# Attention in a macaron block: two heads of a pair on two 64-row tiles of TensorE, and another order of TensorE's work in a unit

## What is computed

```python
q = split(x @ wq.T + bq)
k = split(x @ wk.T + bk)
v = split(x @ wv.T + bv)
scores = jnp.einsum('bhsd,bhtd->bhst', q, k) / scale
scores = jnp.where(causal, scores, -jnp.inf)
weights = jax.nn.softmax(scores, axis=-1)
ctx = jnp.einsum('bhst,bhtd->bhsd', weights, v)
ctx = ctx.transpose(0, 2, 1, 3).reshape(B, S, E)
return ctx @ wo.T + bo
```

```python
x = x + 0.5 * _L0_ffn_ref(_layernorm(x, axis=-1), ...)
x = x + _L0_attn_ref(_layernorm(x, axis=-1), ...)
x = x + 0.5 * _L0_ffn_ref(_layernorm(x, axis=-1), ...)
```

## Time and profile before

| | us |
|---|---|
| median of 3 runs | 1189.49 (1185.66 to 1192.58) |
| span of the profiled execution | 1184.2 |
| TensorE, matmuls busy | 900.6 |
| VectorE busy | 636.2 |
| GpSimd busy | 553.3 |
| ScalarE busy | 487.1 |

### The profile page before, as it was taken

How to read it: one execution, slowest core, us unless ns; L and a number is a source line. 1 busy time by engine, 2 the same in 40 slices (tenths; PEclk the granted TensorE clock), 3 DMA queues, 4 the chain that set the end, 5 groups by cost and what they waited for, 6 DMA issues and landing times. The chain is left out here.

```text
span 1184.2 us, 21961 instructions
## 1 busy us (share of the span) xinstructions
PE 900.6 (76%) x7525; PEld 560.8 (47%) x7525; DVE 636.2 (54%) x1515; ACT 487.1 (41%) x767; POOL 553.3 (47%) x645
## 2 busy tenths in 40 slices
PE   2320899992048999999999799999999622999980
PEld 2320677872023454555555355555554211878770
DVE  6440333331358878878777587787876130333230
ACT  1000343340021676568645477555766301443430
POOL 2775277767510322133427234163323632577776
PEclk9999999997566999999999899999999855999995
DMA  4212676733152114131152302422200113454522
GB/s 146 66 53 84 186 187 158 179 63 28 27 158 47 43 29 149 43 79 45 32 149 67 80 18 58 136 76 63 61 17 13 46 35 113 81 114 69 87 25 19
DMA packets 101649, 92.59 MB, mean 78 GB/s; under 512 B 15348, under 2 KB 80017, under 8 KB 101521
## 3 DMA queue, kind: packets, MB, share of 16 engines
q1 hardware_dynamic: 73024, 71.71, 21.8%
q0 software_dynamic: 27136, 17.09, 10.1%
q10 hardware_dynamic: 1392, 2.51, 0.7%
HBM read 48.32 MB, written 47.12 MB: 81 GB/s over the span
## 5 line engine op out<-in xcount | busy, mean ns | idle before, releaser
L1235 DVE TENSOR_REDUCE m_units<-banks 128x2 f32<-128x512 f32 (+1 forms) x576 | 381.1, 688 | 94.3 <-PE banks L954 78.6
L1184 ACT ACTIVATE pt<-banks 128x1024 f32<-128x1024 f32 (+3 forms) x384 | 291.4, 809 | 163.3 <-PE banks L937 161.4
L954 PE MATMUL banks<-kp,qa 128*128 128x256 bf16 (+1 forms) x1536 | 229.3, 254 | 17.7 <-DMA kp<-k_stack 10.3
L1444 POOL TENSOR_SCALAR_AFFINE_SELECT pt<-pt 128x512 f32<-128x512 f32 x128 | 81.6, 638 | 256.9 <-ACT pt L1184 256.7
L937 PE MATMUL banks<-qb,kp 128*128 128x512 bf16 (+3 forms) x768 | 188.6, 329 | 7.2 <-issue 5.1
L954 PEld LDWEIGHTS banks<-kp,qa 128*128 128x128 bf16 x1536 | 119.5, 99 | 148.7 <-DVE m_units L1235 59.5
L983 PE MATMUL banks<-pt,vs 128*32 128x256 f32 (+2 forms) x2560 | 178.5, 371 | 6.1 <-POOL pt L1444 6.0
L648 ACT ACTIVATE hT<-banks,bfc 128x512 f32<-128x512 f32 (+1 forms) x192 | 113.8, 615 | 168.4 <-DVE bfc L666 94.3
L722 POOL DMA_INDIRECT mid<-ys,ids x80 | 124.9, 1561 | 70.2 <-issue 34.4
L342 POOL DMA_INDIRECT bucket<-rows,row_ix x128 | 125.7, 982 | 64.2 <-issue 38.2
L722 POOL DMA_INDIRECT out_dram<-ys,ids x80 | 123.7, 1546 | 67.8 <-DVE ys L691 32.8
(11 more groups left out here) (166 smaller groups left out, 643.1 us busy)
## 6 DMA issues: line engine op xcount, KB each, us to landing
bucket<-zero SPq DMA_DIRECT2D x16, 660.0 KB, 4.2
xb<-bucket SPq DMA_DIRECT2D x16, 660.0 KB, 4.7
q_stack<-qp SPq DMA_DIRECT2D x24, 256.0 KB, 3.0
k_stack<-kq SPq DMA_DIRECT2D x24, 256.0 KB, 3.7
qa<-q_stack SPq DMA_DIRECT2D x32, 192.0 KB, 3.5
kp<-k_stack SPq DMA_DIRECT2D x32, 192.0 KB, 4.4
qb<-q_stack SPq DMA_DIRECT2D x32, 192.0 KB, 3.4
wfc<-in_L_ffn_c_fc_dram SPq DMA_DIRECT2D x16, 256.0 KB, 3.0
```

The source lines that it names most:

```text
L954: i = nc.tensor.matmul(a_bank[a % 2][:, j * w:(j + 1) * w], qa[par][:, h, qt * P:(qt + 1) * P], kp[g][:, h // 2, k0:k0 + w], start=not dia ...
L1184: nc.scalar.activation(pt[u % PTS][:, 2 * pair:2 * pair + 2, 0:w], two[pair][:, :, 0:w], ACT.Exp, scale=SCALE).then_inc(exp_done[pair], 1)
L1235: nc.vector.tensor_reduce(m_units[:, qt, at, heads[0]:heads[-1] + 1], a_bank[a % 2].rearrange("p (h k) -> p h k", k=w), AX.X, ALU.max).the ...
L1444: nc.gpsimd.affine_select(out=v, in_=v, compare_op=ALU.is_ge, fill=0.0, base=0, pattern=[[0, HS], [1, P]], channel_multiplier=-1).then_inc ...
```

## The change

Two heads of a pair no longer use the full array one after the other with zeros in the other's rows. Each uses its own 64 rows: head s of a pair has rows 64 s to 64 s + 47 (or 50) of both operands. `qa` and `qb` shrink to one slot for a pair, with both heads in it, and their clears go (VectorE's at lines 1368 and 1371). The scores go to the same banks as before. A maxima unit now has one side (`side`, 0 or 1: the upper or lower 64 rows) and both pairs; the causal ones take two query tiles for one side. In a half the full-width ones come first, then the odd ones, then the causal ones, which so all stand in units 6, 7, 10 and 11; there are 36 as before, with as many matmuls of each width. The causal product stays a matmul on all 128 rows. TensorE's order in a unit becomes: both scores, maxima, values half 0, maxima, values half 1, maxima, maxima.

```diff
@@ AUNITS
+    HB = T // 2
     for hf in (1, 0):
-        for qt in range(hf * T // 2, (hf + 1) * T // 2):
+        qts = range(hf * HB, (hf + 1) * HB)
+        for qt in qts:
             for j in range(qt // 2):
-                AUNITS += [(qt, (0, 1), 2 * j * P, 2 * P, False, j), (qt, (2, 3), 2 * j * P, 2 * P, False, j)]
-            if qt % 2:
-                AUNITS.append((qt, range(HS), (qt - 1) * P, P, False, T // 2 - 1))
-            AUNITS.append((qt, range(HS), qt * P, P, True, T // 2))
+                for side in range(2):
+                    AUNITS.append((hf, side, [(qt, 2 * j * P)], 2 * P, False, j))
+        for side in range(2):
+            AUNITS.append((hf, side, [(qt, (qt - 1) * P) for qt in qts if qt % 2], P, False, HB - 1))
+        for q2 in range(hf * HB, (hf + 1) * HB, 2):
+            for side in range(2):
+                AUNITS.append((hf, side, [(q2, q2 * P), (q2 + 1, (q2 + 1) * P)], P, True, HB))
@@ score
-                        i = nc.tensor.matmul(two[pair][:, s, 0:w], kp[g][:, pair, kb * P:(kb + 1) * P],
-                                             qb[par][:, 2 * pair + s, q0:q0 + w], start=True, stop=True)
+                        rows_s = slice(64 * s, 64 * s + KS + 3)
+                        i = nc.tensor.matmul(two[pair][:, s, 0:w], kp[g][rows_s, pair, kb * P:(kb + 1) * P],
+                                             qb[par][rows_s, pair, q0:q0 + w], start=True, stop=True)
@@ maxima
-                        for j, h in enumerate(heads):
-                            i = nc.tensor.matmul(a_bank[a % 2][:, j * w:(j + 1) * w], qa[par][:, h, qt * P:(qt + 1) * P],
-                                                 kp[g][:, h // 2, k0:k0 + w], start=not diag,
+                        rows_s = slice(64 * side, 64 * side + KS)
+                        todo = [(qt, k0, pair) for qt, k0 in segs for pair in range(HS // 2)]
+                        for j, (qt, k0, pair) in enumerate(todo):
+                            i = nc.tensor.matmul(a_bank[a % 2][:, j * w:(j + 1) * w],
+                                                 qa[par][rows_s, pair, qt * P:(qt + 1) * P],
+                                                 kp[g][rows_s, pair, k0:k0 + w], start=not diag,
@@ TensorE's step
+                        for pair in range(2):
+                            score(par, g, b, n, u, pair)
                         for i in range(4):
-                            if i < 2:
-                                score(par, g, b, n, u, i)
-                            elif u >= LAG:
-                                values(par, n, u - LAG, i - 2)
-                            elif not (bt.first and g == 0):
-                                values(1 - par, n - 1, NU - LAG + u, i - 2)
                             if more and a0 + i < a3:
                                 maxima(n + 1, ng, nb, a0 + i, a0 + i + 1)
+                            if i > 1:
+                                continue
+                            if u >= LAG:
+                                values(par, n, u - LAG, i)
+                            elif not (bt.first and g == 0):
+                                values(1 - par, n - 1, NU - LAG + u, i)
@@ VectorE, before attention
-                nc.vector.memset(qa[0][:], 0.0)
                 norm(0)
-                for t_ in qa[1:] + qb:
-                    i = nc.vector.memset(t_[:], 0.0)
-                i.then_inc(cleared, 1)
```

More of the change, by code:

```diff
@@ L748, in macaron_block_kernel @@
             sba = maker(part)
-            qa = [sba(f"qa{i}", [P, HS, S], bf16) for i in range(2)]
-            qb = [sba(f"qb{i}", [P, HS, S], bf16) for i in range(2)]
+            qa = [sba(f"qa{i}", [P, HS // 2, S], bf16) for i in range(2)]
+            qb = [sba(f"qb{i}", [P, HS // 2, S], bf16) for i in range(2)]
             kp = [sba(f"kp{i}", [P, HS // 2, S], bf16) for i in range(NG)]
@@ L830, in load_q @@
                 def load_q(dst, b, g, done):
-                    load_stack(lambda s: dst[64 * s:64 * s + KS].rearrange("p (i s) n -> p s i n", s=2)[:, s],
-                               q_stack, b, g, done)
+                    load_stack(lambda s: dst[64 * s:64 * s + KS], q_stack, b, g, done)
                 def load_k(b, g):
@@ L880, in move @@
                     for s in range(2):
[L881 to L884, removed]
+                        src = max_rows[hf * 3 * HS:(hf + 1) * 3 * HS, :].rearrange("(c s i) n -> s c i n", c=3, s=2)[s]
+                        dst = qb[par][64 * s + KS:64 * s + KS + 3]
+                        sp.dma_start(dst[:, :, hf * HALF:(hf + 1) * HALF], src).then_inc(max_ld[hf][par], 16)
                 def store_stacks(b):
@@ L914, in _ @@
                 wait_apart(sp, stack_st, STORES)
-                wait_apart(sp, cleared, 2)
+                wait_apart(sp, cleared, 1)
                 load_q(qa[0], 0, 0, qa_ld[0])
@@ L944, in maxima @@
                     for a in range(a0, a1):
-                        qt, heads, k0, w, diag, _ = AUNITS[a]
+                        _, side, segs, w, diag, _ = AUNITS[a]
                         if a == 0:
@@ L952, in maxima @@
                                              start=True, stop=False)
-                        for j, h in enumerate(heads):
-                            i = nc.tensor.matmul(a_bank[a % 2][:, j * w:(j + 1) * w], qa[par][:, h, qt * P:(qt + 1) * P],
-                                                 kp[g][:, h // 2, k0:k0 + w], start=not diag,
-                                                 stop=not diag or j == len(heads) - 1)
+                        rows_s = slice(64 * side, 64 * side + KS)
[4 more added lines that the diff above has]
+                                                 kp[g][rows_s, pair, k0:k0 + w], start=not diag,
+                                                 stop=not diag or j == len(todo) - 1)
                         i.then_inc(a_full, 1)
@@ L1099, in _ @@
                     norm_task(pro_at, name, 0)
-                pe.wait_ge(cleared, 2)
+                pe.wait_ge(cleared, 1)
                 maxima(0, 0, 0, 0, NA1 + 4)
@@ L1232, in reduce @@
                 def reduce(n, a):
-                    qt, heads, k0, w, diag, at = AUNITS[a]
+                    hf, side, segs, w, _, at = AUNITS[a]
+                    qt, apart = segs[0][0], segs[-1][0] - segs[0][0]
+                    if apart == 2:
+                        dst = m_units[:].rearrange("p (t o) c h -> p t o c h", o=2)[:, qt // 2:qt // 2 + 2, qt % 2, at]
+                    else:
+                        dst = m_units[:, qt:qt + apart + 1, at]
                     dve.wait_ge(a_full, NA * n + a + 1)
-                    nc.vector.tensor_reduce(m_units[:, qt, at, heads[0]:heads[-1] + 1],
-                                            a_bank[a % 2].rearrange("p (h k) -> p h k", k=w), AX.X,
+                    nc.vector.tensor_reduce(dst[:, :, 2 * side:2 * side + 2],
+                                            a_bank[a % 2].rearrange("p (t h k) -> p t h k", h=2, k=w), AX.X,
                                             ALU.max).then_inc(a_done, 1)
                     if a in (NA1 - 1, NA - 1):
-                        hf = int(a < NA1)
                         wait(dve, parts_ok, 2 * n - hf)
```

## The result

The changed kernel takes 1353.3 us (median of 5 runs, 1342.1 to 1380.3) against 1189.5 us: a ratio of 1.132 (95% interval 1.127 to 1.137). I had forecast 1197.5 us, in a range of 1165 to 1238. The profiled execution is one of the longer ones, with a span of 1373.2 us.

The account below looks back on a forecast made before the run. The attention stage was taken as bound by TensorE's stream, VectorE next. Terms -59 + 14 + 34 + 17 + 7 - 5 - 0.5 make about +8 on 1189.5 us: 1197.5 us, range 1165 to 1238.

Parts of the forecast that it names:

- the last rival: TensorE's clock falls, from more gaps and half its rows idle in the maxima; no time given, chance 0.02.
- Term D: Maxima units, VectorE's cadence: TensorE waits for reductions to free maxima banks, +17 us, bounds +5 to +30.
- E: Chain behind half 1's last maxima unit: TensorE stands still before the transposition of m_parts ending unit 8, +7 us.
- Term A: Attention scores: two 64-row tiles run beside each other, halving the scores' time, -59 us, bounds 0 and -59.
- G: Clears: four clears of 1.76 us leave VectorE, -0.5 us, between -0.8 and 0.
- the rival without overlap: The two score matmuls do not overlap, wanting the same moving or weight path: +47, 1237 us, chance 0.10.
- B: Units 6, 7, 10, 11: value halves split by a maxima unit, four more column-tile visits a group, +14 us.
- C: TensorE's changes between full array and 64-row tiles: 311 new ones at 0.11 us, +34 us, bounds 0 to +44.
- The rival with free changes: Changes between full array and row tiles cost nothing: 1168.5 us, chance 0.18.
- The rivals of slow weight loads: Maxima units: loads slower in a 64-row tile, 1225 us, chance 0.07; or never hidden beside the same rows, 1313, 0.03.
- term F: Today's waits of TensorE for VectorE, mostly at causal maxima of units 8 and 9: half goes away, -5 us.

Follow-up runs that it names:

- e1: The changed kernel with all score and maxima matmuls back on the full array, its new order kept: 1214.2 us, 1.019 of the kernel before.
- e2: The changed kernel with only the maxima back on the full array, scores in row tiles, order kept: 1203.8 us, 1.011 of the kernel before.
- e3: The changed kernel with only the scores back on the full array, maxima in row tiles, order kept: 1260.2 us, 1.061 of the kernel before.
- g1: The changed kernel unaltered, run again on another chip: 1322.3 us, 1.110 of the kernel before.
- e4_fill: The changed kernel plus six unread full-array matmuls of 512 columns before each of 32 waits for m_parts: 1256.7 us, 1.055 of the kernel before.

## Why the prediction was wrong, point by point

**The step that failed is the last rival.** "The clock falls, as TensorE has more gaps and half of its rows idle in the maxima" had a chance of 0.02 and, unlike its neighbours, no time: "each 10 us at half clock costs 5" was never multiplied out, and the sum has the clock at nothing. The reason I gave against it was that "its stalls there are as long as those of terms D and E". I compared single stalls, and the stalls did stay short. What changed is that three things came together: scores in half the time, maxima on half of the rows, and more draining and waiting in units 6 to 8. In the stage the clock is at 0.98 with the last alone (e1) and at 0.96 with it and one of the others (e2, e3); with all three it is 0.65, and 0.72 in g1's profile (380 to 1078 us). That the combination does it is shown; which property of TensorE's work the clock answers to is not.

**What the clock is worth.** Three estimates, all from the runs above and none a run itself. The first is from the changed kernel alone. Its nine runs go from a span of 1276 us at a mean clock of 0.828 to 1379 us at 0.733, which is 439 to 736 us at the lower level (twice what the mean lacks to 1, times the span). A straight line through the nine gives 0.35 us for each microsecond at the lower level and misses none by more than 4 us. Carried on to the 192 us of the kernel before (0.919), far outside the nine, it ends at some 1190 us. The second is from e4_fill, which has the whole change. Without its filling (37 to 41 us, as it covers waits of some 4 us) it would take 1216 to 1220 us. Its stage has 76 of 630 us at the lower level, the kernel before 14 of 562: 62 us more, which cost 22 us at 0.35 each, and 25 to 29 if all of it took 1.66 to 1.9 times as long. That gives 1187 to 1198. The third is e1 plus the differences of e2 and e3, 1250; 314 changes are counted there twice (295 + 330 against 311), 31 us, and the clocks of 0.96 against 0.98 in both cost some 8 to 10 each: 1199 to 1203. So the changed kernel at the clock of the kernel before takes some 1187 to 1203 us; the sum of terms A to G was 1197.5. The other 150 to 166 us are the clock's.

**Term A held.** Four scores in 0.44 us; the rival without overlap is out.

**Terms B and C held, each change by its rows.** A value half alone takes 0.57 us and the way to it 0.10, as before; no run measures B's total by itself. 0.10 between full array and row tile, in the causal product's 0.32 and in e2's and e4's rows alike; I had taken 0.11 from the nearest row, m_parts. The rival with free changes is out. With 311 changes C is 31 instead of 34.

**The rivals of slow weight loads fell.** Four loads of 128 columns into one 64-row tile, and their matmuls, take 0.32 with the change to column tiles behind them (602.01 to 602.33), so some 0.22 of their own, as on the full array (0.22 for a maxima unit). The Trainium skill (TensorE: Matmul & The Clock Gate, "The mechanism" in Part 3) lets loads overlap only with matmuls of other row groups unless they go to the background buffer; in its strict form this case contradicts it, in a row tile as on the full array.

**Term D was nearly right, E too large, where rows show them.** At nearly full clock e2 waits 18.6 us for VectorE over the stage, the kernel before 11.7, and 4.8 for ScalarE instead of 1.5; with term F I had forecast 12 more, and 10 came. For m_parts e2 waits 6.7, the kernel before 3.7: 3 more, where I had 7. In the changed kernel itself a slower TensorE hides both.

**The range** left out the clock because of its chance and not because of its size. A case that costs a seventh of the kernel should have moved the upper end even at 0.1, and I think now that 0.1 was the least it deserved: the change lowers what TensorE does per microsecond in three ways at once.

## What to carry to other kernels

A kernel at TensorE's full clock can lose it by an edit that only makes TensorE's work lighter; the price (here some 0.35 us for each microsecond at the lower level, where a matmul's spacing is 1.66 to 1.9 times as long) is far more than this edit could bring. When an edit shortens or thins TensorE's stream and adds drains or waits, treat the clock as a term of its own, look at the stretch with the least work in it and at what brings the clock back, and try the parts singly and together, since each can be harmless alone. Row tiles pay only where many matmuls follow each other in one tiling: a pair of changes costs 0.20 us, as much as two 512-column scores save when they share the array.

## What I had not expected of the hardware

- Useless matmuls made the kernel faster: 6 x 512 columns in front of each of 32 waits, 41 us of work, 1322 to 1257 us on one chip (clock from 380 to 1000 us 0.73 to 0.94).
- The same filling on 64 rows left the clock at 0.80 instead of 0.94, and gained nothing (1.123 against 1.110 and 1.132 for the changed kernel). The one on all rows was followed by the clock's return within 1 us, five times of five; through those on 64 rows it stayed down for up to 48 us.
- The changed kernel, whose clock goes up and down, varies far more between runs: 1278.0 to 1346.7 us on one chip and 1342.1 to 1380.3 on another, where the kernel before stays within 1%.
- A change between the full array and a 64-row tile costs 0.10 us, though the columns of the array are used alike; two 64-row tiles write to neighbouring banks at full rate beside each other.
